# Grouped-query attention with interleaved projections: the score chunks of a key-value head in one visit or in two

## The chip, the cores and the metric

The kernel runs on one core of one Trainium2 chip. The metric is the device time of one launch in microseconds (us). Three runs of the kernel before gave 704.63, 704.95 and 706.21 us, so its median is 704.95 us.

## What is computed

Three residual layers on a 16 x 64 x 512 tensor. The change touches the first, a cross attention with 32 query heads, 8 key-value heads, head dimension 128, rotary embedding and a causal mask:

```
queries = rope((layernorm(x) @ Wq.T) as 32 heads)
keys    = repeat(rope((ctx @ Wk.T) as 8 heads), 4)
values  = repeat((ctx @ Wv.T) as 8 heads, 4)
scores  = queries . keys / sqrt(128), masked above the diagonal
ctx     = softmax(scores) . values
x       = x + ctx @ Wd.T
```

The causal mask leaves only the first 64 context rows in play, so each of the 16 batches has 64 x 64 scores per query head. Matmuls on wide operands are done as three products of a high and a low part (high x high, high x low, low x high), so one output tile of 512 columns with a contraction of 512 is 12 matmul instructions.

## The kernel before, in words

**Stages.** The keys and values of all heads are projected first and spilled to HBM. Then comes one pass per key-value head g (0 to 7), and after it the self attention and the feed-forward layer, which the change does not touch.

**One head.** `head(g, n, more, first)` exists once for each engine, with the same order of work written out by hand and tied together by semaphores. Head 0 is written out, heads 1 to 5 are a loop on each engine (`Fori(1, NKV - 2)`), head 6 is written out (`more=False`), and head 7 has a tail of its own. During head g, TensorE (PE) does four things in turn:

- the scores of head g, in four chunks of four batches (`scores_x`, L1672 to L1683). One chunk is 16 small matmuls (the profile shows two records for each) into one PSUM bank;
- the query projection of head g + 1, as two halves p = 0, 1 of seven block products each (`product`, L1620 to L1627, a Strassen-like scheme), six matmuls a product. A product is added up in PSUM banks `A_BANK` and `C_BANK`. Below, the first products of half 0 are called by their weights: A-11 (`W_11`), C-12 (`W_12`), A-S2 (`W_S2`), C-S1 (`W_S1`), A-S3 (`W_S3`);
- transposes of the normalised probabilities (`p_transposes`, L1685) and their products with the values (`pv_x`, L1691);
- the output projection of head g, eight tiles of twelve matmuls (`out_x`, L1703).

**PSUM.** There are eight banks: two each of `pj`, `sc`, `tp`, `pv`. `A_BANK` is `pj` 0, `B_BANK` is `pj` 1, `C_BANK` is `tp` 1 and `T_BANK` is `tp` 0. Output tiles 0 to 7 go to B, pv 0, pv 1, B, B, pv 0, pv 1, C.

**The other engines around the scores.** Each score chunk is masked by VectorE (DVE) in `mask_max` (L1229: an add from PSUM, L1232, then a maximum, L1234); GpSimd (POOL) subtracts the maximum (L520); ScalarE (ACT) takes the exponential (L805); DVE sums and takes the reciprocal in `sum_rec` (L1247, L1249); POOL multiplies (L525); PE transposes; ACT copies the transposes out of `T_BANK` (L809). DVE adds a finished output tile to the residual in `out_add` (L1264). On DVE a wait on one of these holds up all that stands behind it, as each engine runs its own program in order.

**The chain that leads to C-S1.** C-12 fills `C_BANK`. DVE adds a copy of the A product to it (`c_mix(0, 0)`, L1140), then multiplies it by the cosines (`t1_q(0, 0)`, L1087). ACT then copies the two halves of the bank, swapped, to SBUF (`turn(0, 0)`, L680 and L681). Only then is `C_BANK` free for C-S1, and PE waits for it: `pe.wait_ge(swp, ri(m, 0) + 1)`, L1747. On DVE, `sum_rec(q + 1, 1)` stands between `c_mix(0, 0)` and `t1_q(0, 0)`.

**Order on PE before (heads 1 to 6).** Output tiles 5, 6, 7 of head g - 1; score chunks 0 and 1; A-11; C-12; score chunks 2 and 3 (into the same two `sc` banks, after chunks 0 and 1 are masked); A-S2; transposes of chunk 0; C-S1; transposes of chunk 1; A-S3; and so on.

**Order on DVE before.** The additions of output tiles 4 to 7 at the end of head g - 1; `mask_max` of chunks 0 and 1; `sum_rec` 0; `c_mix(0, 0)`; `sum_rec` 1; `t1_q(0, 0)`; `mask_max` of chunks 2 and 3.

Of the kernel before, what the change touches and what calls it, by code (L numbers as in the profile page):

```python
# [7 lines left out]
ALU = mybir.AluOpType  # L8
# [4 lines left out]
B, S, D = 16, 64, 512  # L13
# [48 lines left out]
def build(nc, x, ctxT, w_k, w_v, w_q, w_d, w_s, w_o, w_b, w_ag, w_eb, consts, bias_cols, bias_rows, b_thr,  # L62
          kscr, vscr, out):
    es = ExitStack()
    with es:
# [137 lines left out]
        pj, sc, tp, pv = pb("pj"), pb("sc"), pb("tp"), pb("pv")  # L203
# [24 lines left out]
        t1_done, swp, sin_done, rope = sem("t1_done"), sem("swp"), sem("sin_done"), sem("rope")  # L228
        wd_hi, wd_lo = sem("wd_hi"), sem("wd_lo")
        tp_t, tp_c = sem("tp_t"), sem("tp_c")  # L230
        scored, masked, maxed, subbed = sem("scored"), sem("masked"), sem("maxed"), sem("subbed")
# [28 lines left out]

        def by_bank(t, c):
            return t[:, c, :, :].rearrange("p n (a q) -> p a n q", q=S)


        N_SM = 4 * NKV
# [27 lines left out]
        def bs(ap):  # L293
            return ap.rearrange("p (b s) -> p b s", s=S)
# [38 lines left out]
        def ri(m, k):  # L333
            return Q0 + 4 * m + k
# [676 lines left out]
        def _(dve):  # L1011
# [214 lines left out]
            w7_sum(3)  # L1226
            first_add(7, 7)

            def mask_max(n, c):  # L1229
                s3 = bs(sm4[c][:, :])  # L1230
                dve.wait_ge(scored, n + 1)
                dve.tensor_tensor(s3, bs(sc[:, c % 2, :]), mask3, ALU.add).then_inc(masked, 1)  # L1232
                dve.wait_ge(masked, n + 1)
                dve.tensor_reduce(mx[:, c, :], s3, AXX, ALU.max).then_inc(maxed, 1)  # L1234

# [9 lines left out]
            def sum_rec(n, c):  # L1245
                dve.wait_ge(exped, n + 1)
                dve.tensor_reduce(zs[:, c, :], bs(sm4[c][:, :]), AXX, ALU.add).then_inc(summed, 1)  # L1247
                dve.wait_ge(summed, n + 1)
                dve.reciprocal(rz[:, c, :], zs[:, c, :]).then_inc(recd, 1)  # L1249
# [12 lines left out]
            def out_add(g, j, banks=O_BANK):  # L1262
                dve.wait_ge(outx, 8 * g + j + 1)
                dve.tensor_tensor(X[:, j, :], X[:, j, :], banks[j], ALU.add).then_inc(x_done, 1)  # L1264

            def head(g, n, more, first=False):
                q = 4 * g

                def c_mix(p, k):
                    m = 2 * n + p  # L1270
                    if k == 0:
                        c_add(7 * m + 2, 3 * m + 1, C_BANK, pc)
                    elif k == 1:
                        dve.wait_ge(swp, ri(m, 0) + 1)
                        c_add(7 * m + 5, 3 * m + 3, A_BANK, pc, cq[p])
                    else:
                        c_add(7 * m + 7, 3 * m + 2, C_BANK, u2)

                def t1_q(p, k):
                    m = 2 * n + p  # L1280
                    if k == 2:
                        dve.wait_ge(stp, 7 * m + 6)
                        t1_mul(0, ri(m, 2), A_BANK)
                    else:
                        dve.wait_ge(cadd, 3 * m + (0, 1, 0, 2)[k] + 1)
                        t1_mul(k % 2, ri(m, k), cq[p][:, :] if k == 1 else C_BANK)

                mask_max(q, 0)
                mask_max(q + 1, 1)
                if first:  # L1290
                    c_mix(0, 0)
                    t1_q(0, 0)
                    sum_rec(q, 0)
                    sum_rec(q + 1, 1)
                    for i in range(2):
                        dve.wait_ge(s_vs[i], 16 * NVT // 2)
                else:
                    sum_rec(q, 0)
                    c_mix(0, 0)
                    sum_rec(q + 1, 1)  # L1300
                    t1_q(0, 0)
                mask_max(q + 2, 2)
                mask_max(q + 3, 3)
                wd_split(g, 0, wdh, wdl)
                c_mix(0, 1)
                t1_q(0, 1)
                if first:
                    w7_lo(3, 1, 0)
                c_lo(q, 0)
                if first:  # L1310
                    t1_q(0, 2)
                    wd_split(g, 1, wdh, wdl)
                    w7_lo(3, 1, 1)
                else:
                    wd_split(g, 1, wdh, wdl)
                    t1_q(0, 2)
                c_mix(0, 3)
                t1_q(0, 3)
                c_lo(q + 1, 1, sc4)
                out_add(g, 0)  # L1320
                sum_rec(q + 2, 2)
                sum_rec(q + 3, 3)
                out_add(g, 1)
                if more:
                    w7_sum(2 * n + 2)
                else:
                    wd_split(g + 1, 0, wd7h, wd7l)
                c_mix(1, 0)
                t1_q(1, 0)
                out_add(g, 2)  # L1330
                out_add(g, 3)
                c_mix(1, 1)
                t1_q(1, 1)
                c_lo(q + 2, 2)
                t1_q(1, 2)
                c_mix(1, 3)
                t1_q(1, 3)
                c_lo(q + 3, 3, sc4)
                if not more:
                    rope_add_q(0, ri(2 * n + 1, 2), q_out(1, 2))  # L1340
                    rope_add_q(1, ri(2 * n + 1, 3), q_out(1, 3))
                    out_add(g, 4)
                if more:
                    w7_sum(2 * n + 3)
                    out_add(g, 4)
                    out_add(g, 5)
                    out_add(g, 6)
                    out_add(g, 7)

            head(0, 1, True, True)  # L1350
            with dve.Fori(1, NKV - 2) as g:
# [201 lines left out]
        def _(pe):  # L1553
# [115 lines left out]
            for i in range(12, NVT):  # L1669
                v_tile(i)  # L1670

            def scores_x(g, j):  # L1672
                h, c = j // 2, j % 2
                if h == 1:
                    pe.wait_ge(masked, 4 * g + j - 1)
                for b in range(4):
                    bb = 8 * h + 4 * c + b
                    for hp in range(2):
                        blk = (b // 2 * 2 + hp) * 2 + b % 2
                        for r in range(2):  # L1680
                            last = pe.matmul(sc[64 * r:64 * r + 64, c, blk * S:(blk + 1) * S],  # L1681
                                             qr[:, bb, 2 * hp + r, :], kr[:, bb, :], start=True, stop=True)
                last.then_inc(scored, 1)  # L1683

# [6 lines left out]
            def pv_x(g, j, bank=pv):  # L1691
                h, c = j // 2, j % 2
                pe.wait_ge(tp_c, 4 * g + j + 1)
                if c == 0:
                    pe.wait_ge(s_vv[h], 16 * (g + 1))
                for bp in range(2):
                    for bo in range(2):
                        rows, cols = slice(64 * bo, 64 * bo + 64), slice(bp * 256, (bp + 1) * 256)
                        last = pe.matmul(bank[:, bo, cols], vv[rows, 4 * h + 2 * c + bp, :], pt[c][rows, cols],  # L1699
                                         start=True, stop=True)  # L1700
                last.then_inc(pv_t, 1)

            def out_x(g, j, banks=O_BANK, wh=wdh, wl=wdl, first=0, end=REP):  # L1703
                h, i = j // 4, j % 4
                if i % 2 == 0:
                    pe.wait_ge(pv_lo, 4 * g + 2 * h + i // 2 + 1)
                c, at = i // 2, i % 2 * REP
                for r in range(first, end):
                    if j == 0 and r % 2 == 0:
                        pe.wait_ge(wd_lo, 2 * g + r // 2 + 1)  # L1710
                    for part, (a, w) in enumerate(((ch, wh), (cl, wh), (ch, wl))):
                        last = pe.matmul(banks[j], a[:, c, at + r, :], w[:, r, :],  # L1712
                                         start=(r == 0 and part == 0), stop=(r == REP - 1 and part == 2))
                if end == REP:
                    last.then_inc(outx, 1)

            def head(g, n, more, first=False):
# [4 lines left out]
                def added(j):  # L1722
                    pe.wait_ge(x_done, XD0 + 8 * g + j + 1)
# [1 line left out]
                m = 2 * n  # L1725
                pe.wait_ge(rope, Q0 + 6 if first else ri(m, 0))
                pe.wait_ge(s_kr, 16 * (g + 1))
                if not first:
                    pe.wait_ge(pv_lo, 4 * g)
                scores_x(g, 0)  # L1730
                scores_x(g, 1)
                pe.wait_ge(wlo, 2 * m + 1)
                if not first:
                    free(m)
# [3 lines left out]
                product(C_BANK, 0, W_12, X_21, True, True).then_inc(stp, 1)  # L1738
                if first:
                    pe.wait_ge(rope, ri(m, 0))  # L1740
                scores_x(g, 2)
                scores_x(g, 3)
                pe.wait_ge(wlo, 2 * m + 2)
                pe.wait_ge(pcp, 3 * m + 1)
                product(A_BANK, 0, W_S2, X_T2, False, False).then_inc(stp, 1)
# [6 lines left out]
                product(A_BANK, 0, W_S3, X_T3, False, False).then_inc(stp, 1)  # L1752

                added(-2)
                pv_x(g, 0, pv)
                pe.wait_ge(masked, 4 * g + 4)
                pv_x(g, 1, sc)
                pe.wait_ge(cadd, 3 * m + 2)
                product(A_BANK, 0, W_22, X_T4, False, True).then_inc(stp, 1)
# [31 lines left out]
                if more:  # L1791
                    out_x(g, 5)
                    out_x(g, 6)
                    pe.wait_ge(swp, ri(m, 3) + 1)
                    out_x(g, 7)

            head(0, 1, True, True)
            with pe.Fori(1, NKV - 2) as g:
# [388 lines left out]
```

## Time and profile before

| | |
|---|---|
| runs | 704.63, 704.95, 706.21 us; median 704.95 |
| the profiled execution | 706.06 us, of which 704.2 us are the span from its first to its last instruction |
| PE busy | 694.8 us, 99% of the span |
| PE weight loads | 564.0 us, 80%, beside the matmuls |
| DVE busy | 516.4 us, 73% |
| ACT busy | 373.0 us, 53% |
| POOL busy | 471.6 us, 67% |
| DMA | 51.08 MB, mean 73 GB/s |
| granted TensorE clock | 1.000 over the whole span |

Matmuls are pipelined: a record lasts longer than the distance to the start of the next, so starts are compared with starts. "Busy" of PE counts records that overlap as one. A group of records with "x6" is six records merged, with the time from the first's start to the last's end.

### The profile page before, as it was taken

The numbers are of one execution on the slowest core, as the hardware profiler recorded it, in microseconds if no ns is written. First come the engines' busy times: TensorE is split into PE (matmuls) and PEld (weight loads), VectorE is DVE, ScalarE is ACT, GpSimd is POOL, SyncE is SP. The second block draws the span as 40 slices with busy tenths as digits, with TensorE's granted clock in tenths as the row PEclk, the third lists the DMA queues.
The fourth block names the chain that finished last, engine by engine and source line by source line (L and its number), as shares of the span: only waits on it lengthen the run. The fifth ranks groups of instructions, "written<-read, shape, count | busy, mean of one in ns | idle before, by whom it ended". The sixth has DMA issues, their size and how long they took to land.

```text
span 704.2 us, 12879 instructions
## 1 busy us (share of the span) xinstructions
PE 694.8 (99%) x4841; PEld 564.0 (80%) x4841; DVE 516.4 (73%) x815; ACT 373.0 (53%) x560; POOL 471.6 (67%) x360
## 2 busy tenths in 40 slices
PE   8999999899999999999999999999999999999998
PEld 6887888688888888888888888887888888887886
DVE  5566988967767767857758758748668888899734
ACT  6356665634743743753653653654246777665220
POOL 2698155877777778778777877844525799985630
PEclk9999999999999999999999999999999999999999
DMA  7645613140400311310310312200300101011003
GB/s 263 221 150 176 172 46 106 75 164 17 135 31 18 132 35 38 106 45 30 104 45 30 104 45 65 87 16 2 104 2 1 46 31 33 2 47 46 16 1 119
DMA packets 25736, 51.08 MB, mean 73 GB/s; under 512 B 2400, under 2 KB 10720, under 8 KB 25696
## 3 DMA queue, kind: packets, MB, share of 16 engines
q1 hardware_dynamic: 25696, 50.53, 21.8%
q8 instruction: 27, 0.44, 0.3%
q14 instruction: 13, 0.11, 0.1%
HBM read 40.04 MB, written 10.49 MB: 72 GB/s over the span
## 4 chain that ended last, share of the span: by engine, by line
PE 83%; DVE 5%; POOL 4%; DMA 3%; issue 2%; ACT 2%; SPq 1%; DVEq 0%; POOLq 0%; ACTq 0%
PE pj L1625 12%; PE pv L1712 10%; PE pj L1712 10%; PE pj L1816 9%; PE tp L1625 8%; PE sc L1681 4%; PE tp L1712 4%; PE pj L2000 3%; PE pv L1611 3%; PE sc L1866 2%; PE tp L1879 2%; PE pv L1890 2%; PE pv L1699 2%; PE tp L1688 2%; PE sc L1699 2%
## 5 line engine op out<-in xcount | busy, mean ns | idle before, releaser
L496 POOL TENSOR_TENSOR sw<-sw,cst 128x512 f32<-128x512 f32 x72 | 96.9, 1345 | 42.3 <-ACT sw L681 42.0
L520 POOL TENSOR_TENSOR sm<-sm,mx 128x512 f32<-128x512 f32 x64 | 73.0, 1147 | 29.6 <-DVE mx L1234 16.0
L525 POOL TENSOR_TENSOR sm<-sm,rz 128x512 f32<-128x512 f32 x64 | 70.7, 1120 | 27.0 <-DVE rz L1249 27.0
L502 POOL TENSOR_TENSOR qr<-t,sw 128x512 f32<-128x512 f32 x54 | 73.9, 1369 | 7.7
L1625 PE MATMUL tp<-x,w 128*128 128x512 f32 x288 | 74.5, 395 | 0.0
L805 ACT ACTIVATE sm<-sm 128x512 f32<-128x512 f32 x64 | 40.1, 633 | 53.4 <-POOL sm L520 53.1
L514 POOL TENSOR_TENSOR w<-raw,w 128x896 fp32r<-128x896 f32 x24 | 50.3, 2118 | 26.0 <-ACT w L658 26.0
L1816 PE MATMUL pj<-xh,ws 128*128 128x512 f32 x192 | 64.6, 402 | 0.2 <-ACT kb L899 0.2
L1625 PEld LDWEIGHTS tp<-x,w 128*128 128x128 f32 x288 | 53.0, 188 | 10.8
L658 ACT ACTIVATE w<-raw 128x1792 fp32r<-128x1792 f32 x15 | 25.6, 1705 | 59.7 <-DVE raw L1109 59.7
L1625 PE MATMUL pj<-xt,w 128*128 128x512 f32 x192 | 51.7, 407 | 0.0
L1625 PE MATMUL pj<-x,w 128*128 128x512 f32 x192 | 50.6, 399 | 0.4 <-DVE w L1132 0.4
L1247 DVE TENSOR_REDUCE zs<-sm 128x8 f32<-128x512 f32 x64 | 42.7, 666 | 6.9 <-ACT sm L805 6.6
L680 ACT ACTIVATE sw<-tp 64x512 f32<-64x512 f32 x36 | 21.5, 596 | 41.4 <-DVE t L1087 29.8
L1625 PEld LDWEIGHTS pj<-xt,w 128*128 128x128 f32 x192 | 33.9, 188 | 10.6 <-issue 4.6
L1816 PEld LDWEIGHTS pj<-xh,ws 128*128 128x128 f32 x192 | 36.0, 188 | 7.9 <-ACT kb L899 0.6
L1625 PEld LDWEIGHTS pj<-x,w 128*128 128x128 f32 x192 | 34.9, 188 | 8.4 <-DVE w L1132 0.9
L1712 PE MATMUL pv<-wdh,ch 128*128 128x512 f32 x104 | 40.5, 389 | 0.0
L1712 PE MATMUL pv<-wdh,cl 128*128 128x512 f32 x104 | 40.5, 389 | 0.0
L1712 PE MATMUL pv<-wdl,ch 128*128 128x512 f32 x104 | 40.5, 389 | 0.0
L1611 PE MATMUL pv<-wv,cxh 128*128 128x512 f32 x128 | 39.6, 390 | 0.0
L1712 PE MATMUL pj<-wdh,ch 128*128 128x512 f32 x92 | 36.2, 394 | 1.8 <-DVE wdl L1259 1.2
(279 smaller groups left out, 1849.6 us busy)
## 6 DMA issues: line engine op xcount, KB each, us to landing
rawd<-in_w_d SPq DMA_DIRECT2D x16, 512.0 KB, 3.4
raw<-in_w_q SPq DMA_DIRECT2D x15, 512.0 KB, 3.3
kscr<-sm SPq DMA_DIRECT2D x16, 256.0 KB, 2.1
vscr<-sm SPq DMA_DIRECT2D x16, 256.0 KB, 2.6
kr<-kscr SPq DMA_DIRECT2D x8, 512.0 KB, 3.2
vv<-vscr SPq DMA_DIRECT2D x16, 256.0 KB, 3.5
raw<-in_w_v SPq DMA_DIRECT2D x4, 512.0 KB, 3.9
X<-in_x SPq DMA_DIRECT2D x4, 512.0 KB, 6.8
```

The costliest lines, as they stand in the source:

```text
L496: pool.tensor_tensor(bs(sw[par][:, :]), bs(sw[par][:, :]), rep(cst[:, C_SIN:C_SIN + S], HB), ALU.mult).then_inc(sin_done, 1)
L502: pool.tensor_tensor(o, bs(t1[par][:, :]), bs(sw[par][:, :]), ALU.add).then_inc(rope, 1)
L514: pool.tensor_tensor(w7[p][:, 1, c], raw8[:, 1:8, :].rearrange("p n c -> p (n c)")[:, c], w7[p][:, 0, c].bitcast(F32), ALU.subtract).then_ ...
L520: pool.tensor_tensor(s3, s3, per_group(mx[:, c, :], 8), ALU.subtract).then_inc(subbed, 1)
L525: pool.tensor_tensor(s3, s3, per_group(rz[:, c, :], 8), ALU.mult).then_inc(normed, 1)
L805: act.activation(sm4[c][:, :], sm4[c][:, :], ACT.Exp, scale=scale).then_inc(exped, 1)
L1247: dve.tensor_reduce(zs[:, c, :], bs(sm4[c][:, :]), AXX, ALU.add).then_inc(summed, 1)
L1611: last = pe.matmul(pv[:, vi % 2, :], a[:, k, tok], wv[gg][:, r, k, :], start=(k == 0 and part == 0), stop=(k == KT - 1 and part == 2))
L1625: last = pe.matmul(bank, a, r, start=(start and k == 0 and part == 0), stop=(stop and k == 1 and part == 2), skip_group_check=True)
L1681: last = pe.matmul(sc[64 * r:64 * r + 64, c, blk * S:(blk + 1) * S], qr[:, bb, 2 * hp + r, :], kr[:, bb, :], start=True, stop=True)
L1712: last = pe.matmul(banks[j], a[:, c, at + r, :], w[:, r, :], start=(r == 0 and part == 0), stop=(r == REP - 1 and part == 2))
L1816: last = pe.matmul(pj[:, k % 2, :], ws[t][:, part // 2, i, c], (xl if part == 1 else xh)[:, i, tok], start=(m == 0), stop=(m == 3 * KT - 1))
```

## The change

Heads 1 to 6 get another order. On PE, all four score chunks of head g come in one visit, before output tile 7 of head g - 1, which follows them. Chunks 0 and 1 go to the two `sc` banks as before, chunk 2 to `pj` 1 (`B_BANK`) and chunk 3 to `pv` 0; before these two, PE waits for the additions of output tiles 4 and 5. The two chunks that stood between C-12 and A-S2 are gone from there, and the wait for `masked` moves ahead of `pv_x(g, 0)`, which writes `pv` 0. On DVE, `mask_max` of chunks 0, 1, 2 comes first, then `out_add` of tile 7 of head g - 1, then `mask_max` of chunk 3, then `sum_rec` 0, `c_mix(0, 0)`, `sum_rec` 1, `t1_q(0, 0)`. Head 0 and head 7 keep their scores as they were.

```diff
+        SC_FIRST = [sc[:, 0, :], sc[:, 1, :], sc[:, 0, :], sc[:, 1, :]]
+        SC_LOOP = [sc[:, 0, :], sc[:, 1, :], pj[:, 1, :], pv[:, 0, :]]
...
-            def mask_max(n, c):
+            def mask_max(n, c, banks=SC_FIRST):
                 s3 = bs(sm4[c][:, :])
                 dve.wait_ge(scored, n + 1)
-                dve.tensor_tensor(s3, bs(sc[:, c % 2, :]), mask3, ALU.add).then_inc(masked, 1)
+                dve.tensor_tensor(s3, bs(banks[c]), mask3, ALU.add).then_inc(masked, 1)
...
-                mask_max(q, 0)
-                mask_max(q + 1, 1)
                 if first:
+                    mask_max(q, 0)
+                    mask_max(q + 1, 1)
                     c_mix(0, 0)
                     t1_q(0, 0)
                     sum_rec(q, 0)
                     sum_rec(q + 1, 1)
                     for i in range(2):
                         dve.wait_ge(s_vs[i], 16 * NVT // 2)
+                    mask_max(q + 2, 2)
+                    mask_max(q + 3, 3)
                 else:
+                    for c in range(3):
+                        mask_max(q + c, c, SC_LOOP)
+                    out_add(g - 1, 7)
+                    mask_max(q + 3, 3, SC_LOOP)
                     sum_rec(q, 0)
                     c_mix(0, 0)
                     sum_rec(q + 1, 1)
                     t1_q(0, 0)
-                mask_max(q + 2, 2)
-                mask_max(q + 3, 3)
                 wd_split(g, 0, wdh, wdl)
...
                     out_add(g, 6)
-                    out_add(g, 7)
...
-            def scores_x(g, j):
+            def scores_x(g, j, banks=SC_FIRST):
                 h, c = j // 2, j % 2
-                if h == 1:
+                if h == 1 and banks is SC_FIRST:
                     pe.wait_ge(masked, 4 * g + j - 1)
...
-                            last = pe.matmul(sc[64 * r:64 * r + 64, c, blk * S:(blk + 1) * S],
+                            last = pe.matmul(banks[j][64 * r:64 * r + 64, blk * S:(blk + 1) * S],
...
-                if not first:
+                if first:
+                    scores_x(g, 0)
+                    scores_x(g, 1)
+                else:
                     pe.wait_ge(pv_lo, 4 * g)
-                scores_x(g, 0)
-                scores_x(g, 1)
+                    scores_x(g, 0, SC_LOOP)
+                    scores_x(g, 1, SC_LOOP)
+                    added(-4)
+                    scores_x(g, 2, SC_LOOP)
+                    added(-3)
+                    scores_x(g, 3, SC_LOOP)
+                    pe.wait_ge(swp, ri(m - 1, 3) + 1)
+                    out_x(g - 1, 7)
                 pe.wait_ge(wlo, 2 * m + 1)
...
                 if first:
                     pe.wait_ge(rope, ri(m, 0))
-                scores_x(g, 2)
-                scores_x(g, 3)
+                    scores_x(g, 2)
+                    scores_x(g, 3)
...
                 added(-2)
+                pe.wait_ge(masked, 4 * g + 4)
                 pv_x(g, 0, pv)
-                pe.wait_ge(masked, 4 * g + 4)
                 pv_x(g, 1, sc)
...
                     out_x(g, 6)
-                    pe.wait_ge(swp, ri(m, 3) + 1)
-                    out_x(g, 7)
```

## Rows read from the trace of the kernel before

**Rows 1.** The page: PE's busy time; the chain that ended last, by engine.
```profile
PE 694.8 (99%) x4841; PEld 564.0 (80%) x4841; DVE 516.4 (73%) x815; ACT 373.0 (53%) x560; POOL 471.6 (67%) x360
...
PE 83%; DVE 5%; POOL 4%; DMA 3%; issue 2%; ACT 2%; SPq 1%; DVEq 0%; POOLq 0%; ACTq 0%
```

**Rows 2.** Two stretches: length, busy PE, PEld, DVE, ACT, POOL, granted clock, DMA share, GB/s.
```profile
118.00:143.00 25.00, 22.27 (x214) 17.11 (x211) 24.01 (x29) 16.38 (x24) 18.06 (x13) 1.00 0.29 91
...
224.50:276.00 51.50, 51.50 (x357) 41.89 (x356) 37.04 (x50) 27.03 (x38) 39.27 (x29) 1.00 0.18 61
```

**Rows 3.** Timeline of PE, from head 2 to head 3: start, duration, line, out<-in.
```profile
273.14 0.39 PE L1712 MATMUL pv<-wdl,ch 128*128 128x512 f32 x1
...
275.86 0.39 PE L1712 MATMUL tp<-wdl,ch 128*128 128x512 f32 x1
276.18 2.08 PE L1681 MATMUL sc<-kr,qr 128*64 128x64 f32 x64
278.19 1.66 PE L1625 MATMUL pj<-x,w 128*128 128x512 f32 x6
279.69 1.52 PE L1625 MATMUL tp<-x,w 128*128 128x512 f32 x6
...
283.15 1.66 PE L1625 MATMUL pj<-x,w 128*128 128x512 f32 x6
284.65 0.60 PE L1688 MATMUL tp<-cst,sm 128*128 128x128 f32 x4
285.06 1.65 PE L1625 MATMUL tp<-x,w 128*128 128x512 f32 x6
286.55 0.60 PE L1688 MATMUL tp<-cst,sm 128*128 128x128 f32 x4
286.90 1.64 PE L1625 MATMUL pj<-xt,w 128*128 128x512 f32 x6
```

**Rows 4.** Timeline of DVE over the same boundary; in brackets idle time before, and its releaser.
```profile
272.77 0.68 DVE L1264 TENSOR_TENSOR X<-X,pj 128x512 f32<-128x512 f32 x1
273.37 1.27 DVE L1264 TENSOR_TENSOR X<-X,pv 128x512 f32<-128x512 f32 x2
276.29 0.69 DVE L1264 TENSOR_TENSOR X<-X,tp 128x512 f32<-128x512 f32 x1 [1.65 <-PE tp L1712]
277.38 0.69 DVE L1232 TENSOR_TENSOR sm<-sc,cst 128x512 f32<-128x512 f32 x1 [0.40 <-PE sc L1681]
278.11 0.69 DVE L1234 TENSOR_REDUCE mx<-sm 128x8 f32<-128x512 f32 x1
278.71 0.68 DVE L1232 TENSOR_TENSOR sm<-sc,cst 128x512 f32<-128x512 f32 x1
...
281.34 0.20 DVE L1249 RECIPROCAL rz<-zs 128x8 f32<-128x8 f32 x1
281.58 0.70 DVE L1140 TENSOR_TENSOR tp<-tp,pc 128x512 f32<-128x512 f32 x1
282.19 0.67 DVE L1247 TENSOR_REDUCE zs<-sm 128x8 f32<-128x512 f32 x1
...
283.01 0.68 DVE L1087 TENSOR_TENSOR t<-tp,cst 128x512 f32<-128x512 f32 x1
```

**Rows 5.** Timeline of ACT: the two swapped copies that free C_BANK.
```profile
283.81 0.59 ACT L680 ACTIVATE sw<-tp 64x512 f32<-64x512 f32 x1 [0.96 <-DVE t L1087]
284.41 0.59 ACT L681 ACTIVATE sw<-tp 64x512 f32<-64x512 f32 x1
```

**Rows 6.** Timeline of POOL over the same boundary.
```profile
271.01 1.55 POOL L502 TENSOR_TENSOR qr<-t,sw 128x512 f32<-128x512 f32 x1
274.75 4.17 POOL L514 TENSOR_TENSOR w<-raw,w 128x896 fp32r<-128x896 f32 x2 [2.18 <-ACT w L658]
...
281.62 1.04 POOL L525 TENSOR_TENSOR sm<-sm,rz 128x512 f32<-128x512 f32 x1 [0.39 <-DVE rz L1249]
```

**Rows 7.** Timeline of PE at the start of the kernel.
```profile
1.43 3.69 PE L1631 MATMUL pv<-x 128*128 128x512 f32 x9 [1.43 <-POOL x L481]
```

## The prediction, made before the change was run

> **What bounds the kernel now.** I read the page first: PE is busy for 99% of the span and carries 83% of the chain that ended last [rows 1]. So time falls only where PE spends less, and grows by whatever PE is made to wait. Then the stretches: over one whole head of the loop (51.50 us from one score visit to the next) PE is busy for all 51.50 us at a granted clock of 1.00, while DVE has 37, ACT 27 and POOL 39 us of work [rows 2]. There is no idle time on PE in which a new wait could disappear, and the rest of a head cannot catch up on a delay. Last the timelines over one boundary between heads, since six heads (1 to 6) repeat it. On PE [rows 3] the reader should see two things. A visit to the scores costs more than its matmuls. And C-S1 starts at 285.06, only 0.06 after ACT's second swapped copy ends at 284.41 + 0.59 = 285.00 [rows 3, 5]. The chain that frees `C_BANK` is already just in time; in the order before, chunks 2 and 3 stand between its two ends and fill it.
>
> **Part 1, one visit instead of two: a gain.** Ordinary matmuls start 0.227 apart (six matmuls of C-12 take 1.52 to the last end: 5 x 0.227 + 0.39). From the last matmul ahead of the visit (275.86) to C-12 (279.69) are 3.83 us; without a visit it would be 7 x 0.227 = 1.59. A visit thus costs 2.24 us. In it, 64 records start over 2.08 - 0.22 = 1.86 us (the last is some 0.22 long), 32 pairs at 0.059; 32 more pairs in the same visit cost 1.89. The change drops the difference, 2.24 - 1.89 = 0.35 us a head: the slower start of the visit (0.32 after the matmul before instead of 0.227) and the slow start of what follows (1.66 for six instead of 1.52) [rows 3]. The trace shows this price at each change of matmul shape. The Trainium skill ("TensorEngine Tiling (Array Packing)", Key Properties) says that changing the tiling mode drains TensorE; by that rule one of two drains goes, which is the 0.35, and it is no larger because the rows hold the whole switch. The two new waits within the visit could eat some of it, so it is bounded by 0 and 0.35; I take 0.35, as those waits are long fulfilled: output tiles 4 and 5 are added by 272.77 + 0.68 = 273.45 and about 274.05 [rows 4], and chunks 2 and 3 want them at about 275.4 and 276.3.
>
> **Part 2, the visit is earlier by one output tile: nothing.** It needs the last rotary addition of the head before, which ends at 271.01 + 1.55 = 272.56 [rows 6]; PE would want it at 273.46. Cover 0.9 us; a later one would cost what is beyond. A-11 needs the weight splits of POOL, which end at 278.92 [rows 6] while A-11 moves to 280.2. SP's reload of the keys waits for the last score and so starts some 6 us earlier, in a queue with little to move (DMA share 0.18 [rows 2]).
>
> **Part 3, what stood between C-12 and C-S1 is gone: a loss.** I place the new order on the same clock. Tile 6 starts its last matmul at 273.14. Scores from 273.46; last record 1.86 + 1.89 later, 277.21; tile 7 from 277.36 (0.15 later, as 278.19 follows the visit), with its slow start 2.86 to A-11 at 280.22; C-12 1.36 later at 281.58; A-S2 at 282.94; transposes of chunk 0 at 284.30; and C-S1 could start 0.35 later, as 286.90 follows 286.55 [rows 3], at 284.65. That is 0.41 before today's 285.06: the 0.35, and the 0.06 that it waits today.
>
> Now the chain. C-12 ends 1.52 after its start, at 283.10, and DVE sees it a little later (tile 7's addition starts 0.04 after that tile's last matmul ends, 276.29 against 276.25 [rows 3, 4]; I take 0.1): 283.2. The steps after that have rows: from the start of the mix to the start of the cosine product 283.01 - 281.58 = 1.43 (mix, sum and reciprocal of chunk 1), from there to the first swapped copy 0.80, from there to C-S1 1.25 [rows 3 to 5]: 3.48 in all. C-S1 starts at 286.7 at the earliest. PE has only A-S2 and four transposes to put in between, 3.07 us from C-12's start, against 1.52 + 0.1 + 3.48 = 5.1. PE stands for 2.05 us.
>
> Is DVE there at 283.2? Its masks start 1.20 after the visit does (277.38 against 276.18), at 274.66, when the additions of tiles 5 and 6 are just done (273.37 + 1.27 = 274.64). Each mask and maximum takes 1.33 (277.38 to 278.71) [rows 4], so three end at about 278.7. Then DVE waits for tile 7, whose last matmul ends at about 280.3, and idles for 1.6 us with chunk 3 and the sums queued behind it. Addition 280.37, mask and maximum of chunk 3 from 280.98, sum of chunk 0 from 282.3, reciprocal to 283.2, mix at 283.25. So DVE is late by 0.05 at most, and the stand becomes 2.1 us. The exponentials are no limit: POOL is free at 278.92 and has subtracted twice by about 281.1 (1.04 each, as its multiplication [rows 6]), and the exponential of chunk 1 is wanted only at 283.9. The normalisation of chunk 0 takes 1.04 on POOL [rows 6] and ends at 284.3, as the transposes want it. After C-S1 the copies on ACT follow as today, shifted with it; the transposes of chunk 1 and A-S3 come 1.49 and 1.84 us after C-S1 as today (286.55 and 286.90 [rows 3]), behind copies that follow the swap at once. Nothing later gives the delay back, as PE is full.
>
> **Sum.** C-S1 moves from 285.06 to 286.75, so 2.1 - 0.35 - 0.06 = 1.67 to 1.69 us a head, and six heads (five of the loop and head 6): 10.0 us. The profiled execution took 706.06 us, its span 704.2, and it becomes about 716 with a span of 714.2; it lies 1.1 above the median of 704.95, which is the one that I move: **715.0 us**.
>
> **Rivals.** (a) *Faster, 702.9 us.* The C_BANK chain hides and only Part 1 is left: 704.95 - 6 x 0.35. For it speaks that the gain is in the rows; it needs about 1.6 us between the end of C-12 and C-S1 where the trace has 285.06 - 281.21 = 3.85 [rows 3] and the sum of fixed steps 3.5. It decides at the wait ahead of C-S1: from 0.41 us of standing on (0.35 and today's 0.06), the change loses. DVE work that I place there wrongly could shorten it, nothing that I see removes two copies of 0.59 on ACT and two operations of 0.7 on DVE [rows 4, 5], 2.6 us. (b) *The clock falls at the new stand, 724.7 us.* In the stretch from 118 to 143, PE was idle for 2.73 us in a few waits and the granted clock stayed 1.00 [rows 2]. At the start of the kernel nine matmuls took 3.69 us, 0.41 apart instead of 0.227 [rows 7], which is what the lower level, 1.2 GHz, would give, though the row of the clock does not say so. If each stand brought nine such matmuls, that is 9 x 0.18 = 1.6 us a head more. The Trainium skill ("TensorE: Matmul & The Clock Gate", HAM oscillation) has idle gaps of PE throttle its clock; the trace has not shown it for waits of this size so far. (c) *DVE turns out the later one.* Its order puts tile 7 ahead of chunk 3, so whatever delays tile 7 or a mask by x delays the mix by x. Each 0.3 us is 1.8 us in all: 716.8. (d) *No change*, 705: the stand is only as long as the saving; needs a chain of 1.8 us, against all rows.
>
> **How the numbers follow.** A measurement of this kernel can tell about 0.2% (1.4 us) from no change. My forecast, with (c) as its upper part, has 0.90; (b) 0.03; (a) 0.05; (d) 0.02. The range: at the low end the mix and the cosine product start without the small distances between operations (0.4 us less): (1.67 - 0.4) x 6 = 7.6, 712.6. At the high end no gain in Part 1 (+0.35) and DVE 0.25 late: 2.27 x 6 = 13.6, 718.6; both together are unlikely, so 718.3. Faster is (a), 0.05; same is (d), 0.02; slower the rest, 0.93.
>
> **What would show it.** In the profile of the changed kernel: 128 score records in one group, starting in six places and 2.7 us earlier; A-S2 following C-12 directly; an idle time of about 2 us on PE ahead of C-S1, ended by ACT L681's line; an idle time of about 1.6 us on DVE ahead of the addition of tile 7; heads of about 53.2 us instead of 51.55; clock 1.00. It is wrong if C-S1 has no idle time before it, or if heads keep 51.5 us or less.

## The result: 718.81 us, 2.0% slower, and the profile after

| | before | changed |
|---|---|---|
| median of five runs | 704.95 us (704.57 to 706.6) | 718.81 us (718.49 to 720.49) |
| ratio | | 1.0195, 95% interval 1.0176 to 1.0214 |
| profiled execution, its span | 706.06, 704.2 us | 718.64, 716.6 us |
| mean granted clock | 1.000 | 0.995 |

Below, *stand* means the idle time of PE ahead of C-S1, and a *fall* a stretch in which the granted clock of TensorE goes down to 0.50. The sign was as forecast; the size was not: 13.9 us against 10.0, and the time lies 0.5 us above the range. The page of the changed kernel, its span, busy time, and chain that ended last by engine, against [rows 1]:

```profile
span 716.6 us, 12874 instructions
...
PE 698.0 (97%) x4841; PEld 566.3 (79%) x4841; DVE 520.5 (73%) x815; ACT 372.9 (52%) x560; POOL 470.1 (66%) x360
...
PE 78%; DVE 9%; POOL 3%; issue 3%; DMA 3%; ACT 2%; SPq 1%; DVEq 0%; ACTq 0%; POOLq 0%
```

PE's share of the chain falls from 83 to 78%, and DVE's rises from 5 to 9%. The timeline of PE over the first boundary of the new order (head 0 to head 1), to be read against [rows 3]:

```profile
169.27 0.39 PE L1719 MATMUL pv<-wdl,ch 128*128 128x512 f32 x1
169.59 2.08 PE L1688 MATMUL sc<-kr,qr 128*64 128x64 f32 x64
171.50 1.10 PE L1688 MATMUL pj<-kr,qr 128*64 128x64 f32 x32
172.44 1.10 PE L1688 MATMUL pv<-kr,qr 128*64 128x64 f32 x32
173.47 0.50 PE L1719 MATMUL tp<-wdh,ch 128*128 128x512 f32 x1
...
176.32 1.52 PE L1632 MATMUL pj<-x,w 128*128 128x512 f32 x6
177.68 1.52 PE L1632 MATMUL tp<-x,w 128*128 128x512 f32 x6
179.04 1.52 PE L1632 MATMUL pj<-x,w 128*128 128x512 f32 x6
180.55 0.66 PE L1695 MATMUL tp<-cst,sm 128*128 128x128 f32 x4
182.90 1.67 PE L1632 MATMUL tp<-x,w 128*128 128x512 f32 x6 [1.69 <-ACT sw L685]
184.41 0.60 PE L1695 MATMUL tp<-cst,sm 128*128 128x128 f32 x4
...
186.33 1.14 PE L1706 MATMUL pv<-pt,vv 64*128 64x256 f32 x8
```

All four chunks come in one visit (3.88 us to the first matmul of tile 7, forecast 3.90), then tile 7, A-11, C-12, A-S2, the transposes of chunk 0, and then 1.69 us of idle time ahead of C-S1, ended by ACT's swapped copy. DVE over the same boundary, against [rows 4]:

```profile
176.52 0.69 DVE L1268 TENSOR_TENSOR X<-X,tp 128x512 f32<-128x512 f32 x1 [1.69 <-PE tp L1719]
177.13 0.68 DVE L1236 TENSOR_TENSOR sm<-pv,cst 128x512 f32<-128x512 f32 x1
177.85 0.69 DVE L1238 TENSOR_REDUCE mx<-sm 128x8 f32<-128x512 f32 x1
178.45 0.68 DVE L1251 TENSOR_REDUCE zs<-sm 128x8 f32<-128x512 f32 x1
179.16 0.20 DVE L1253 RECIPROCAL rz<-zs 128x8 f32<-128x8 f32 x1
179.41 0.70 DVE L1144 TENSOR_TENSOR tp<-tp,pc 128x512 f32<-128x512 f32 x1
180.02 0.68 DVE L1251 TENSOR_REDUCE zs<-sm 128x8 f32<-128x512 f32 x1
...
180.85 0.69 DVE L1091 TENSOR_TENSOR t<-tp,cst 128x512 f32<-128x512 f32 x1
```

C-12 ends at 177.68 + 1.52 = 179.20, the mix starts at 179.41 and C-S1 at 182.90, so from mix to C-S1 are 3.49 us (forecast 3.48). The other two stretches to read are those of whole heads (from visit to visit) and of the clock, against [rows 2]; columns as there:

```profile
169.59:222.86 53.27, 51.58 (x357) 41.80 (x356) 37.67 (x52) 26.95 (x39) 38.94 (x28) 1.00 0.18 60
222.86:277.70 54.84, 53.15 (x358) 43.05 (x357) 37.43 (x51) 27.09 (x39) 38.96 (x28) 0.97 0.17 57
277.70:332.54 54.84, 53.15 (x357) 43.04 (x356) 37.40 (x51) 27.11 (x39) 38.96 (x28) 0.97 0.16 57
332.54:385.79 53.25, 51.56 (x358) 41.82 (x357) 37.72 (x52) 27.03 (x39) 38.98 (x28) 1.00 0.17 59
236.63:240.05 3.42, 3.42 (x12) 2.74 (x11) 0.00 (x0) 1.63 (x4) 3.28 (x4) 0.50 0.42 153
```

A head is 53.25 to 53.27 us, which is 51.55 + 1.7, or 54.84. In the two long ones (heads 2 and 3) the granted clock was 0.50, the lower level of 1.2 GHz, for 3.42 us. In head 2 that stretch begins 0.46 us after C-S1 does, at 236.63. PE's timeline there:

```profile
236.17 2.56 PE L1632 MATMUL tp<-x,w 128*128 128x512 f32 x6 [1.69 <-ACT sw L685]
238.52 1.06 PE L1695 MATMUL tp<-cst,sm 128*128 128x128 f32 x4
239.23 2.02 PE L1632 MATMUL pj<-xt,w 128*128 128x512 f32 x6
241.17 1.14 PE L1706 MATMUL pv<-pt,vv 64*128 64x256 f32 x8
```

The same idle time of 1.69 us, but then six matmuls take 2.56 us where they took 1.67 in head 1. From C-S1 to the value products it is 241.17 - 236.17 = 5.00 us, where head 1 has 186.33 - 182.90 = 3.43. One fall costs 1.57 us. Head 6 is not like the five others: its stand is shorter, and no fall follows.

```profile
452.08 1.66 PE L1632 MATMUL tp<-x,w 128*128 128x512 f32 x6 [1.42 <-ACT sw L685]
```

So the spans add up. Five heads from visit to visit took 439.04 - 169.59 = 269.45 us, against 5 x 51.55 = 257.75: 11.7 more, of which 2 x 1.57 = 3.1 are falls. Head 6 lost about another 1.4: up to the first visit of head 7 it took 489.43 - 439.04 = 50.39 us, against 477.00 - 430.83 = 46.17 and the 2.8 of tile 7, which now comes behind the visit. Together some 13.1, of which 10.0 are stands less the saving of the visit, and 3.1 the clock. The work ahead of head 0, which the change does not touch, happened to be 0.7 us quicker (its scores start at 117.07 against 117.80), and the spans differ by 12.4.

### The profile page after: what moved, and what is told of

Its sections match the earlier page's. It is cut to its first block, busy times and chain, and to the rows that moved or that the text cites. A ratio compares the mean times of both kernels' runs of the same rounds, so it can differ in the third digit from the quotient of the medians.

```text
span 716.6 us, 12874 instructions
## 1 busy us (share of the span) xinstructions
PE 698.0 (97%) x4841; PEld 566.3 (79%) x4841; DVE 520.5 (73%) x815; ACT 372.9 (52%) x560; POOL 470.1 (66%) x360
## 4 chain that ended last, share of the span: by engine, by line
PE 78%; DVE 9%; POOL 3%; issue 3%; DMA 3%; ACT 2%; SPq 1%; DVEq 0%; ACTq 0%; POOLq 0%
PE pv L1719 10%; PE pj L1719 10%; PE pj L1632 9%; PE pj L1830 9%; PE tp L1632 8%; PE tp L1719 4%; PE pj L2014 3%; PE pv L1618 3%; PE sc L1880 2%; PE tp L1893 2%; PE pv L1904 2%; PE sc L1688 2%; PE pv L1706 2%; PE tp L1695 2%; PE sc L1706 2%
## 5 line engine op out<-in xcount | busy, mean ns | idle before, releaser
L1632 PE MATMUL tp<-x,w 128*128 128x512 f32 x288 | 76.5, 403 | 9.9 <-ACT sw L685 9.9
L506 POOL TENSOR_TENSOR qr<-t,sw 128x512 f32<-128x512 f32 x54 | 72.1, 1336 | 7.7
L1632 PE MATMUL pj<-x,w 128*128 128x512 f32 x192 | 49.0, 391 | 0.4 <-DVE w L1136 0.4
L1144 DVE TENSOR_TENSOR cq<-pj,pc 128x512 f32<-128x512 f32 x15 | 10.4, 692 | 46.1 <-PE pj L1632 46.1
```

The costliest lines, as they stand in the source:

```text
L506: pool.tensor_tensor(o, bs(t1[par][:, :]), bs(sw[par][:, :]), ALU.add).then_inc(rope, 1)
L1632: last = pe.matmul(bank, a, r, start=(start and k == 0 and part == 0), stop=(stop and k == 1 and part == 2), skip_group_check=True)
```

## The experiments

Eight runs, in two groups; within a group all ran on one chip, with the kernel before beside them (705.45 us in the first, 705.30 in the second).

**1. A shorter chain.** The changed kernel with the sum of chunk 1 behind the cosine product:

```diff
                     c_mix(0, 0)
-                    sum_rec(q + 1, 1)
                     t1_q(0, 0)
+                    sum_rec(q + 1, 1)
```

> Edit: the changed kernel, with sum_rec of chunk 1 on DVE moved behind the cosine product t1_q(0, 0), so that the chain from C-12 to C-S1 is one sum and one reciprocal shorter (0.82 us). Theory (PE stands for that chain, and the granted clock falls behind some of the stands, which makes up what the forecast lacked): the stand ahead of C-S1 goes from 1.6 to 0.8 us in each of six heads, a head without a fall takes 52.45 us instead of 53.27, and the time is 718.8 - 6 x 0.82 = 713.9, or about 710.5 if with the shorter stand no clock falls are left. Rival 1 (DVE is late because it waits for output tile 7 ahead of chunk 3, and the chain behind C-12 is not what counts): the mix starts when it starts now, nothing of the order behind it matters, 718.8. Rival 2 (the extra time comes with the new banks or the merged visit): 718.8 too.

Measured: 712.17 us (711.96 to 712.22), ratio 1.0091 (1.0078 to 1.0104), clock 1.000 in all five runs; 713.9 or 710.5 was expected. DVE and PE in this kernel's timeline:

```profile
179.20 0.70 DVE L1144 TENSOR_TENSOR tp<-tp,pc 128x512 f32<-128x512 f32 x1
180.04 0.69 DVE L1091 TENSOR_TENSOR t<-tp,cst 128x512 f32<-128x512 f32 x1
```

```profile
180.34 0.65 PE L1695 MATMUL tp<-cst,sm 128*128 128x128 f32 x4
182.09 1.66 PE L1632 MATMUL tp<-x,w 128*128 128x512 f32 x6 [1.10 <-ACT sw L685]
```

DVE still waits for tile 7 as long as before (1.69 us of idle time), and the mix comes at the same place, so rival 1 is out: only the order behind the mix was touched, and the time fell by 6.6 us. Rival 2 wanted 718.8 too; runs 3 and 8 test it directly. From mix to cosine product it is 0.84 us now instead of 1.44, 0.60 less where I had reckoned 0.82 less: the product now waits for the mix's own result, which the sum used to cover. A head (from visit to visit, 169.38 to 222.14) is 52.76 us, only 0.50 less: the transposes of chunk 1 come 0.05 later behind C-S1 than before (183.65) and A-S3 0.11 later (184.06), as POOL's normalisation of chunk 1, whose sum now stands behind the product, ends only at 183.59. Six times 0.50 is 3.0; the other 3.6 us are put down to the falls, of which none is left with an idle time of 1.10 us.

**2. The stand filled with work.** The changed kernel with nine idle matmuls (nobody reads their result) where PE stands:

```diff
                 product(A_BANK, 0, W_S2, X_T2, False, False).then_inc(stp, 1)
+                if not first:
+                    for _ in range(9):
+                        pe.matmul(T_BANK, w7[0][:, 0, 0:P], x7b(X_T2, 0)[:, 0, :], start=True, stop=True)
                 p_transposes(g, 0)
```

> Edit: the changed kernel, with nine idle matmuls of 128 x 512 (9 x 0.227 = 2.04 us) into T_BANK between A-S2 and the transposes of chunk 0, in heads 1 to 6, where PE would otherwise stand; their results are overwritten. Theory: the chain to C-S1 is as long as before, so each head without a fall keeps its 53.27 us, but PE isn't idle, so the clock doesn't fall: 715.0 (704.95 + 6 x 1.67), granted clock 1.000 all through. Rival (the clock falls for another reason, or costs nothing): 718.8 with the same low stretches; or, if matmuls are added where PE has no time, 718.8 + up to 12.

Measured: 715.63 us (715.57 to 716.59), ratio 1.0145 (1.0129 to 1.0161), clock 0.999 to 1.000 in four runs. The timeline of PE, and one head (columns as in [rows 2]):

```profile
180.30 2.21 PE L1764 MATMUL tp<-x,w 128*128 128x512 f32 x9
182.35 0.60 PE L1695 MATMUL tp<-cst,sm 128*128 128x128 f32 x4
182.80 1.64 PE L1632 MATMUL tp<-x,w 128*128 128x512 f32 x6
```

```profile
222.74:275.99 53.25, 53.25 (x367) 43.57 (x366) 37.68 (x51) 27.01 (x39) 38.97 (x28) 1.00 0.18 59
```

Work that nobody needs makes the kernel 3.2 us faster. The head is as long as in the changed kernel, 53.25 us, with PE now busy for all of it, and no fall; what brings the mean clock of this profile to 0.999 is the last microsecond of the kernel (0.63 from 712.5 on), when PE has no work left. This splits the 13.9 us: about 10 are the stands (10.2 over the kernel before beside it), as forecast, and 3 to 4 are the clock behind them.

**3. The banks alone.** The order of before, with chunks 2 and 3 in `pj` 1 and `pv` 0:

```diff
-                    mask_max(q + 2, 2)
-                    mask_max(q + 3, 3)
+                    mask_max(q + 2, 2, SC_LOOP)
+                    mask_max(q + 3, 3, SC_LOOP)
...
-                scores_x(g, 2)
-                scores_x(g, 3)
+                    scores_x(g, 2, SC_LOOP)
+                    scores_x(g, 3, SC_LOOP)
```

> Edit: the order of the kernel before on PE and DVE (two score visits, tile 7 ahead of them), with only the banks of the change: chunks 2 and 3 go to pj 1 and pv 0. Theory: banks alone cost nothing and there is no new stand, 705.0 within 0.7, clock 1.000. Rival 2 (the new banks are what makes it slow): the larger part of the 13.9 us, 712 to 719.

Measured: 705.5 us (704.94 to 708.56), ratio 1.0005 (0.9992 to 1.0018), heads of 51.54 and 51.55 us. So the banks cost nothing, which is half of rival 2; the merged visit, its other half, is cleared by run 8. One thing does not fit: in two of the twelve runs, which took 707.95 and 708.56 us, the mean clock was 0.998 and 0.997, though this kernel has no stand ahead of C-S1. No trace of these two was kept, so where the clock was low in them is not known.

**4. A stand in the old order.** The kernel before with three idle reductions in the chain, heads 1 to 6:

```diff
                     sum_rec(q + 1, 1)
+                    for o in (mv[:, :, 0], mv[:, :, 1], stats[:, :, 0]):
+                        dve.tensor_reduce(o, bs(cq[0][:, :]), AXX, ALU.max)
                     t1_q(0, 0)
```

> Edit: the kernel before, with three idle reductions of 128 x 512 (0.67 us each) on DVE between sum_rec of chunk 1 and the cosine product in heads 1 to 6, so that the old order gets a stand of about 2.0 us ahead of C-S1. Theory: 6 x 2.0 = 12 us for the stands, and the clock falls behind some of them, at about 1.6 us each: 717 to 724, with low stretches of the clock behind C-S1. Rival (the falls belong to the new order, banks or visit, not to the stand): 717.0 and a clock of 1.000. If a stand on PE could be made up later in the head: below 715.

Measured: 715.99 us (715.72 to 716.82), ratio 1.0149 (1.0133 to 1.0165), clock 1.000 in all four runs:

```profile
181.27 0.60 PE L1690 MATMUL tp<-cst,sm 128*128 128x128 f32 x4
183.40 1.69 PE L1627 MATMUL tp<-x,w 128*128 128x512 f32 x6 [1.53 <-ACT sw L681]
```

The old order gets slower by the same mechanism, with heads of 53.26 us, and gives nothing back. But the falls that I expected (717 to 724 us) did not come. The idle time was 1.53 us (1.31 in head 6), less than the 1.69 of the changed kernel. Either the falls need the longer idle time, or they belong to the new order. Runs 5 to 7 are for this.

**5. The changed kernel again.** No edit.

> The changed kernel as it is, beside the others on one chip. Theory: 718.8, clock below 1.000 in most runs, low stretches behind C-S1 in some of the heads, whose number differs from run to run; heads without one 53.27 us, with one 54.84. Rival (what was low in the first runs was the chip): 715.5 with a clock of 1.000.

Measured: 719.93 us (717.22 to 721.65), ratio 1.0219 (1.0205 to 1.0233). The mean clock of its five runs was 0.998, 0.995, 0.993, 0.991 and 0.993, at spans of 715.3, 717.6, 719.2, 719.8 and 717.9. The profiled run had one fall, in the first of these two heads:

```profile
382.87:437.69 54.82, 53.12 (x357) 43.03 (x356) 37.44 (x51) 27.13 (x39) 38.96 (x28) 0.97 0.17 57
329.62:382.87 53.25, 51.56 (x358) 41.81 (x357) 37.69 (x51) 27.01 (x39) 39.02 (x28) 1.00 0.18 59
```

A fall of 3.42 us at half clock takes 1.71 off a mean over some 717 us, 0.0024. By this reckoning the five means stand for about 1, 2, 3, 4 and 3 falls; only the first was profiled, and it shows the one. Its five stands of 1.69 to 1.70 us (heads 1 to 5) are alike, and one of them brought a fall: same stand, other outcome. The rival, that the low clock of the first runs was the chip's, is out.

**6. Two idle matmuls.** The edit of run 2 with `range(2)`: PE's pause is split, C-S1 starts no sooner.

> Edit: the changed kernel with two idle matmuls (0.45 us) into T_BANK between A-S2 and the transposes of chunk 0, in heads 1 to 6; the stand goes from 1.6 to 1.15 us of idle time, and C-S1 starts when it does now. Theory (the falls belong to the idle time ahead of C-S1, since a stand of 1.80 from start to start brought none in the old order and one of 1.96 did in the new one): no falls, 715.6. Rival (the falls belong to the new order or to the sparse matmuls of the whole stretch, which two idle ones hardly change): low stretches remain, 717 to 719.

Measured: 716.81 us (715.25 to 717.13), ratio 1.0156 (1.0142 to 1.017), clock 1.000 in all five runs:

```profile
181.91 0.62 PE L1764 MATMUL tp<-x,w 128*128 128x512 f32 x2
182.37 0.60 PE L1695 MATMUL tp<-cst,sm 128*128 128x128 f32 x4
184.40 1.66 PE L1632 MATMUL tp<-x,w 128*128 128x512 f32 x6 [1.43 <-ACT sw L685]
```

The new order, with 1.43 us of idle time in place of 1.69 (1.16 in head 6), has no fall. (The idle time shrank by 0.26, not by 0.45, in part because the transposes, which started 0.15 late before, now wait for nothing.) Its median is 1.2 us over that of run 2 though the heads are alike (53.25 and 53.27); its profiled run reached head 0 about 1.3 us later, in a part that none of the edits touches.

**7. A longer stand in the old order.** The edit of run 4 with a fourth reduction.

> Edit: the kernel before with four idle reductions in the chain in place of three, so that the stand is some 2.45 us from start to start. Theory (it is the stand that brings the falls, in whatever order): 716.0 + 6 x 0.62 = 719.7 and on top of it falls of 1.6 us each in some heads, 721 to 729, clock below 1.000. Rival (the falls belong to the new order): 719.7 and a clock of 1.000.

Measured: 722.43 us (722.01 to 724.43), ratio 1.0254 (1.0238 to 1.027), clock 0.993 to 0.995 in all five runs:

```profile
342.37 0.60 PE L1690 MATMUL tp<-cst,sm 128*128 128x128 f32 x4
345.12 2.69 PE L1627 MATMUL tp<-x,w 128*128 128x512 f32 x6 [2.15 <-ACT sw L681]
...
454.24 2.57 PE L1627 MATMUL tp<-x,w 128*128 128x512 f32 x6 [1.90 <-ACT sw L681]
```

```profile
172.18:226.02 53.84, 51.72 (x357) 41.90 (x356) 39.38 (x54) 27.00 (x38) 39.28 (x29) 1.00 0.17 59
333.89:389.38 55.49, 53.34 (x358) 43.15 (x357) 39.38 (x54) 26.99 (x38) 39.02 (x29) 0.97 0.17 57
345.50:348.90 3.40, 3.40 (x12) 2.74 (x11) 1.99 (x3) 1.47 (x4) 3.13 (x3) 0.50 0.08 16
```

Here is the fall in the order of before, with the old banks and two visits: the same 3.4 us at 0.50, at C-S1, in two of six heads, once behind 2.15 us of idle time (head 4) and once behind 1.90 (head 6). So it belongs to the idle time ahead of C-S1 and not to the new order.

**8. Tile 7 in the gap.** One visit kept, and the hole behind C-12 filled with the work that was put ahead of it:

```diff
+        OT_BANK = [None] * 7 + [T_BANK]
...
                     scores_x(g, 3, SC_LOOP)
-                    pe.wait_ge(swp, ri(m - 1, 3) + 1)
-                    out_x(g - 1, 7)
...
-                added(-1)
+                if first:
+                    added(-1)
                 product(C_BANK, 0, W_12, X_21, True, True).then_inc(stp, 1)
+                if not first:
+                    out_x(g - 1, 7, OT_BANK)
...
                 product(A_BANK, 0, W_S2, X_T2, False, False).then_inc(stp, 1)
+                if not first:
+                    added(-1)
                 p_transposes(g, 0)
...
-                    for c in range(3):
+                    for c in range(4):
                         mask_max(q + c, c, SC_LOOP)
-                    out_add(g - 1, 7)
-                    mask_max(q + 3, 3, SC_LOOP)
-                    sum_rec(q, 0)
                     c_mix(0, 0)
-                    sum_rec(q + 1, 1)
+                    sum_rec(q, 0)
                     t1_q(0, 0)
+                    sum_rec(q + 1, 1)
+                    out_add(g - 1, 7, OT_BANK)
...
-                if first:
-                    part_copy(pc, 14 * n + 1, A_BANK)
+                part_copy(pc, 14 * n + 1, A_BANK)
                 exp(q, 0, X_SCALE)
-                if not first:
-                    part_copy(pc, 14 * n + 1, A_BANK)
...
-                    act.wait_ge(stp, 14 * n + 2)
-                    wdhi(g, 0, wdh)
                     turn(0, 0)
                     p_copy(q, 0)
                     part_copy(u2, 14 * n + 3, A_BANK)
+                    wdhi(g, 0, wdh)
```

> Edit: the changed kernel's single visit kept, but output tile 7 goes to T_BANK and stands between C-12 and A-S2, where the two chunks stood; on DVE the order is four masks, mix, sum 0, cosine product, sum 1, addition of tile 7; on ACT the copy of A comes first and the weight copy for the output projection behind the copy of A-S2. Theory: the place behind C-12 is covered by tile 7 (2.72 us), A-S2 and the transposes, 4.4 us against a chain that is now some 3.3 us, so there is no stand, and only the saving of the visit is left, with the 0.06 of waiting: heads of 51.14 us, 705.4 - 6 x 0.41 = 703.0, clock 1.000. Rival (the masks and sums of four chunks in a row are a new wait ahead of the transposes of chunk 0, which need POOL's normalisation): a stand of up to 1 us there, 705 to 709.

Measured: 703.68 us (702.57 to 705.07), ratio 0.9977 (0.9967 to 0.9987): the only version faster than the kernel before, by 1.6 us where 2.5 were expected. PE's timeline behind C-12, and a head:

```profile
277.52 1.52 PE L1628 MATMUL tp<-x,w 128*128 128x512 f32 x6
...
281.60 1.53 PE L1628 MATMUL pj<-x,w 128*128 128x512 f32 x6
282.96 0.60 PE L1691 MATMUL tp<-cst,sm 128*128 128x128 f32 x4
283.32 1.64 PE L1628 MATMUL tp<-x,w 128*128 128x512 f32 x6
```

```profile
221.03:272.14 51.11, 51.11 (x357) 41.84 (x356) 37.84 (x51) 26.87 (x39) 38.90 (x28) 1.00 0.18 62
```

C-S1 follows the transposes by 0.36 us, which is no wait. The head is 51.11 us, 0.44 less than before: the saving of the merged visit and the small wait that stood ahead of C-S1. In the profiled run the six heads are together 2.6 us shorter; why the medians differ by less is not known. The rival's new wait ahead of the transposes isn't there.

## Why the prediction was wrong, point by point

- **Part 1, the saving of one visit (0.35 us a head): right.** The visit takes what was worked out, and run 8, which has the one visit and no stand, has heads 0.44 us shorter, against 0.41 forecast. The two new waits within the visit cost nothing: 171.50 and 172.44 follow at the pitch of the rest.
- **Part 2, the earlier visit: right.** Nothing waits ahead of the scores (they follow by 0.32 us as before).
- **Part 3, the stand ahead of C-S1: right in place, cause and size.** The chain from mix to C-S1 is 3.49 us against 3.48, the head without a fall 53.25 us against 53.22. Counted as the forecast counts it, from 0.35 us after the start of the transposes, the stand is 2.00 us (182.90 - 180.90) against 2.1; the 1.69 of the profile counts from their end. Run 1 moved it by cutting the chain, run 4 made it in the old order. That the sum comes to 10.0 us as forecast is in a small part luck: five heads lost 1.71 us each, against 1.67, and head 6 only 1.4.
- **Rival (c), DVE late behind tile 7: did not come.** DVE does idle for 1.69 us behind tile 7 (forecast 1.6), yet the mix starts 0.2 us after C-12 ends.
- **The step that failed: the clock, rival (b), at 0.03.** The sum put the clock behind the stands at nothing, on the ground that PE's idle 2.73 us in the stretch from 118 to 143 had left it at 1.00 [rows 2]. But that idle time was four waits, and the row sums them; the longest was 1.20 us, shorter than any stand of the changed kernel:

```profile
139.10 0.50 PE L1712 MATMUL pj<-wdh,ch 128*128 128x512 f32 x1 [1.20 <-DVE wdl L1259]
```

Each of the first five stands of the changed kernel is a single idle time of 1.69 us, and behind two of them in the first profile, and one in the second, the clock fell; the mean clocks of the other runs (0.990 to 0.998) stand for one to four falls each. The rival had the fall in every head, 9.7 us, and the forecast in none; it lies between. The price of one fall, 1.6 us against 1.57, is near in part by luck: the nine slow matmuls were carried over from the start of the kernel, where the clock's own row says 1.00, and no row said that a stand would bring nine. The Trainium skill ("TensorE: Matmul & The Clock Gate", HAM oscillation), cited there, tells of idle gaps that throttle TensorE; the traces agree that this happens, but behind gaps shorter than those it tells of. The missing term is 1.57 us times two to three falls, 3 to 5 us; without it, in run 2, the time is 715.63, where 715.0 was forecast.

What stays open: why of stands of the same length some bring a fall and others not, whether the two matmuls of run 6 help by shortening the idle time or by their own work, and where the clock was low in the two slower runs of run 3. No run was made for it.

## What to carry to other kernels

When work is moved on a saturated engine, look at the place that it leaves: here it covered a chain through two other engines, and the stand it left cost almost six times (2.0 us against 0.35) what the merged visit saved. Where a stand is unavoidable, fill part of it: a wait of 1.7 us on TensorE cost nearly as much again (1.57 us) through the clock in some of its places, and useless matmuls gave 3 us back. The gain of a merge is kept when something as long, and independent of the chain, takes the vacated place, as tile 7 did in run 8.

## What the hardware showed that was not expected

- Behind a single idle time of 1.69 to 1.70 us on PE the granted clock went to 0.50 (1.2 GHz) for 3.42 us in three of the ten such places of two profiles, at 1.57 us each. In the old order of work (run 7) it did so behind one of five idle times of 2.12 to 2.15 us, and behind one of 1.90. It did so nowhere in the profiles of runs 4, 6 and 1, whose stands are at most 1.54, 1.44 and 1.10 us long, and the mean clock of the 4, 5 and 5 runs of these kernels was 1.000 throughout.
- One such fall in some 717 us shows as 0.998 in the mean clock, but that mean takes in the whole span: the last microsecond of run 2, without work for PE, was enough for 0.999.
- The cosine product, which reads from PSUM what the mix has just written there, starts 0.84 us after the mix does when it stands right behind it, where an operation that does not need the mix starts 0.61 after (run 1: 179.20 to 180.04; changed kernel: 179.41 to 180.02). The maximum of a chunk, which reads its mask's result from SBUF, pays less: it starts 0.72 us after the mask (177.13 to 177.85). So the sum and reciprocal of chunk 1 (0.68 and 0.20 us) delay the product by only 0.60 us (1.44 against 0.84).
